# One third of a convolution moved to VectorE, seven taps instead of six on TensorE, and later copies of a projection in the prologue of a hybrid state-space block

## The reference

```python
xz = x @ in_proj_w.T                     # x group-normalised
xh, z = jnp.split(xz, 2, axis=-1)        # 192 channels each
xc = silu(conv3x3_depthwise(xh) + conv_b)
xs = [by rows, by columns, and both reversed]        # K = 4 directions
x_dbl = einsum('bkdl,kcd->bkcl', xs, x_proj_w)       # 24 + 16 + 16 rows
dts, Bs, Cs = split(x_dbl)
dts = softplus(einsum('bkrl,kdr->bkdl', dts, dt_projs_w) + dt_projs_b)
out_y = selective_scan(xs, dts, -exp(A_logs), Bs, Cs, Ds)
...
# then norm, gate by silu(z), projection, residual; linear attention; routed experts
```

## Time and profile before

| what | value |
|---|---|
| median of 3 runs | 2322.05 us (2319.41 to 2322.06) |
| the profiled execution | 2317.98 us, span 2316.2 us |
| busy over the span: PE, DVE, ACT, POOL | 87%, 68%, 50%, 56% |
| mean granted TensorE clock | 0.96 |
| the prologue | the first 283 us of the span |

### The profile page before, as it was taken

One profiled execution on the slowest core, in us unless ns is written; L12 is line 12 of the kernel. 1 busy time (PEld: TensorE's weight loads), 2 busy tenths in 40 slices (PEclk: granted clock), 3 DMA queues, 4 the chain that ended last, 5 costly groups with the idle time before them and its releaser, 6 DMA issues.

```text
span 2316.2 us, 20220 instructions
## 1 busy us (share of the span) xinstructions
PE 2019.9 (87%) x5878; PEld 934.3 (40%) x5878; DVE 1572.6 (68%) x1477; ACT 1153.9 (50%) x1251; POOL 1299.7 (56%) x467
## 2 busy tenths in 40 slices
PE   7997488888888888888888888779995999999997
PEld 3432133333333333333333333355662555555554
DVE  7697989999999999999999999453554000000000
ACT  4777766766667666676676766111111211111111
POOL 0100089999999999999999999301223111111110
PEclk9996589999999999999999999889997999999999
DMA  5545542222422224222232220510323433333300
GB/s 182 176 151 202 202 115 72 74 73 59 118 72 73 72 61 116 73 72 72 63 100 72 72 73 9 222 41 22 110 88 136 154 118 119 122 119 122 122 24 6
DMA packets 79203, 228.84 MB, mean 99 GB/s; under 512 B 10880, under 2 KB 37106, under 8 KB 77745
## 3 DMA queue, kind: packets, MB, share of 16 engines
q1 hardware_dynamic: 73008, 211.25, 28.4%
q0 software_dynamic: 6144, 16.98, 2.1%
HBM read 166.10 MB, written 64.03 MB: 99 GB/s over the span
## 4 chain that ended last, share of the span: by engine, by line
PE 47%; DVE 22%; issue 17%; POOL 8%; ACT 3%; DMA 1%; DVEq 0%; SPq 0%; ACTq 0%; POOLq 0%
DVE arena L1581 14%; PE ps L1375 11%; PE ps L1363 11%; PE ps L1116 6%; POOL arena L559 4%; POOL arena L542 4%; PE ps L1311 3%; PE ps L1100 2%; PE ps L1017 2%; PE ps L1045 2%; DVE ps L1564 1%; PE ps L1113 1%; PE ps L1262 1%; PE ps L1057 1%; PE ps L1300 1%
## 5 line engine op out<-in xcount | busy, mean ns | idle before, releaser
L559 POOL TENSOR_TENSOR arena<-arena 128x2048 f32<-128x2048 f32 x192 | 867.5, 4527 | 22.3 <-DVE arena L1581 18.4
L1116 PE MATMUL ps<-arena 128*128 128x512 f32 x1536 | 726.7, 595 | 29.0 <-POOL arena L559 28.9
L1581 DVE TENSOR_TENSOR_SCAN arena<-arena,ps 128x1024 f32<-128x1024 f32 x264 | 587.7, 2266 | 2.1 <-issue 2.1
L825 ACT ACTIVATE arena<-ps 128x1024 f32<-128x1024 f32 x384 | 390.7, 1018 | 255.9 <-PE ps L1100 248.1
L1100 PE MATMUL ps<-arena 96*128 (+1 forms) x1296 | 367.1, 385 | 133.9 <-DVE arena L1581 112.7
L1116 PEld LDWEIGHTS ps<-arena 128*128 128x128 f32 x1536 | 288.5, 190 | 288.4 <-issue 192.9
L542 POOL TENSOR_TENSOR arena<-arena 128x1024 f32<-128x1024 f32 x120 | 282.9, 2358 | 104.5 <-DMA arena<-b_rows 104.5
L1860 DVE TENSOR_TENSOR arena<-ps,arena 128x384 f32<-128x384 f32 x32 | 17.8, 557 | 449.1 <-PE ps L1375 449.1
L1564 DVE TENSOR_TENSOR ps<-ps,arena 128x1024 f32<-128x1024 f32 x264 | 309.1, 1216 | 16.0 <-PE ps L1100 15.9
L817 ACT ACTIVATE arena<-arena 128x1024 f32<-128x1024 f32 x264 | 300.8, 1139 | 8.9 <-DVE arena L1581 8.4
L1100 PEld LDWEIGHTS ps<-arena 96*128 96x128 bf16 x1296 | 112.9, 98 | 465.9 <-DVE arena L1581 215.7
(11 more groups left out here) (210 smaller groups left out, 1666.3 us busy)
## 6 DMA issues: line engine op xcount, KB each, us to landing
arena<-b_rows SPq DMA_DIRECT2D x240, 256.0 KB, 4.2
arena<-in_w SPq DMA_DIRECT2D x16, 2304.0 KB, 13.3
delta<-arena SPq DMA_DIRECT2D x24, 512.0 KB, 2.6
delta_x<-arena SPq DMA_DIRECT2D x24, 512.0 KB, 2.6
arena<-delta SPq DMA_DIRECT2D x24, 512.0 KB, 3.6
arena<-delta_x SPq DMA_DIRECT2D x24, 512.0 KB, 4.8
slot_in<-arena SPq DMA_DIRECT2D x8, 772.0 KB, 8.1
arena<-slot_in SPq DMA_DIRECT2D x8, 772.0 KB, 18.3
```

Of the source, the lines that this page charges most:

```text
L559: nc.gpsimd.tensor_tensor(hst[:, h:h + 2], hst[:, h:h + 2], c_sb[:, c:c + 2], ALU.mult).then_inc(p2_ok, 2)
L825: nc.scalar.activation(c_sb[:, u % RING], C_PS, ACT.Copy).then_inc(c_free, 1)
L1116: mm = pe.matmul(Y_PS[:, h * 512:(h + 1) * 512], ident, hst[:, u % HRING, h * 512:(h + 1) * 512], start=False, stop=(u == UN - 1))
L1581: nc.vector.tensor_tensor_scan(h, f, x, 0.0, ALU.mult, ALU.add).then_inc(sc_ok, 1)
```

## The change

It touches the prologue alone. Third 0 of pair 1 is convolved whole by VectorE (`first_third`), right behind pair 0's taps and around the first split, into the tile that `last_row` wrote before. TensorE's `conv` is left with thirds 1 and 2, of which it does seven taps, and VectorE's `last_taps` the remaining two. `x_proj(1, 0)` and its `split_hi` and `split_rest` stand ahead of the end of pair 0. `split_hi`, `split_rest`, `split_mid` and `split_lo` of the other projections stand one step later; TensorE's projections keep their steps. ScalarE does the three `conv_out` of pair 1 together, with one change of tables and one back instead of two and two. `FILL_ORDER` follows.

```diff
-TAPS, PE_TAPS = 9, 6
+TAPS, PE_TAPS = 9, 7
...
-for j in range(J):
-    FILL_ORDER += [("x", 0, j + 1), ("conv", 1, j)]
+FILL_ORDER += [("x", 0, 1), ("conv", 1, 1), ("x", 0, 2), ("x", 0, 3), ("conv", 1, 2)]
...
-CONV_AT = {1: (0, 0), 2: (0, 1), 4: (1, 0), 5: (1, 1), 7: (2, 0), 8: (2, 1)}
-LAST_ROW_AT = {2: 0, 5: 1, 8: 2}
-TWO_THIRDS_AT, LAST_THIRD_AT = 6, HALVES - 2
+CONV_AT = {1: (1, 0), 4: (1, 1), 7: (2, 0), 8: (2, 1)}
+LAST_TAPS_AT = {5: 1, 8: 2}
+SILU_AT, NEXT_PAIR_AT = HALVES - 3, HALVES - 2
+FAR_THIRD = place(3, 0) + 1
...
 # SP
-                    if i % J == 1 and i // J + 1 < K:
+                    if i % J == 2 and i // J + 1 < K:
                         store_parts(p, i // J + 1)
...
 # ScalarE
-                if p:
-                    split_hi(p, 0)
-                    split_mid(p, 0)
...
-                    if k < K and s % J == 0:
+                    if k < K and s % J == 1:
                         split_hi(p, k)
-                    if k < K and s % J == 1:
+                    if k < K and s % J == 2:
                         split_mid(p, k)
-                    if p == 0 and s == TWO_THIRDS_AT:
+                    if p == 0 and s == SILU_AT:
                         nc.scalar.preload_act_table_set("silu_and_others")
-                        conv_out(1, 0)
-                        conv_out(1, 1)
+                        for j in range(J):
+                            conv_out(1, j)
...
+                    if p == 0 and s == HALVES - 1:
+                        split_hi(1, 0)
+                    if p == 1 and s == 0:
+                        split_mid(1, 0)
...
 # TensorE
-                if p:
-                    x_proj(p, 0)
                 delta_product(p, 0)
...
+                    if p == 0 and s == NEXT_PAIR_AT:
+                        x_proj(1, 0)
...
 # VectorE
+            def first_third(first, last):
+
+                acc = xy[:, OJ, :].rearrange("p (h w) -> p h w", w=HW)
+                if first == 0:
+                    dve.wait_ge(xh_ok, FAR_THIRD)
+                    chain.link(nc.vector.tensor_scalar(acc, xpad[:, 0, 0:HW, 0:HW], conv_w[:, 0, 0:1], None, ALU.mult))
+                    first = 1
+                for tap in range(first, last):
+                    dy, dx = divmod(tap, 3)
+                    ins = nc.vector.scalar_tensor_tensor(out=acc, in0=xpad[:, 0, dy:dy + HW, dx:dx + HW], scalar=conv_w[:, 0, tap:tap + 1],
+                                                         in1=acc, op0=ALU.mult, op1=ALU.add)
...
-            for j in range(J):
+            for j in range(1, J):
                 for tap in range(PE_TAPS):
...
+            first_third(0, 7)
+            split_rest(0, 0)
+            first_third(7, 8)
+            split_lo(0, 0)
+            first_third(8, TAPS)
             for p in range(NP):
-                split_rest(p, 0)
-                split_lo(p, 0)
                 for s in range(HALVES + 1):
...
-                    if k < K and s % J == 0:
-                        split_rest(p, k)
                     if s >= 1:
                         finish(p, s - 1)
                     if k < K and s % J == 1:
+                        split_rest(p, k)
+                    if k < K and s % J == 2:
                         split_lo(p, k)
-                    if p == 0 and s in LAST_ROW_AT:
-                        last_row(LAST_ROW_AT[s])
+                    if p == 0 and s in LAST_TAPS_AT:
+                        last_taps(LAST_TAPS_AT[s])
+                    if p == 0 and s == HALVES - 1:
+                        split_rest(1, 0)
+                    if p == 1 and s == 0:
+                        split_lo(1, 0)
```

More of the change, by code:

```diff
@@ L200, in hybrid_block_kernel @@
         rw = Region(arena, PRO, COLS)
-        z_sb, xpad, conv_diag = rw.take(J, S), rw.take(J, PADW, PADW), rw.take(J, PE_TAPS, P)
+        z_sb, xpad, conv_diag = rw.take(J, S), rw.take(J, PADW, PADW), rw.take(J - 1, PE_TAPS, P)
         tap_sum = rw.take(2, S)
@@ L1029, in conv @@
                     mm = pe.matmul(slot[:, h * 512:(h + 1) * 512].rearrange("p (h w) -> p h w", w=HW),
-                                   conv_diag[:, j, tap], xpad[:, j, y0:y0 + HW // 2, dx:dx + HW],
+                                   conv_diag[:, j - 1, tap], xpad[:, j, y0:y0 + HW // 2, dx:dx + HW],
                                    start=(tap == 0), stop=(tap == PE_TAPS - 1))
@@ L1450, in taps, with last_taps @@
                         chain.link(ins)
-            def last_row(j):
+            def first_third(first, last):
[8 more added lines that the diff above has]
+                                                         in1=acc, op0=ALU.mult, op1=ALU.add)
+                    if tap == TAPS - 1:
+                        ins.then_inc(conv_ok, 1)
+                    else:
+                        chain.link(ins)
+            def last_taps(j):
                 slot = fill_slot("conv", 1, j).rearrange("p (h w) -> p h w", w=HW)
-                dve.wait_ge(cpe_ok, j + 1)
+                dve.wait_ge(cpe_ok, j)
                 for tap in range(PE_TAPS, TAPS):
@@ L1521, in _ @@
             nc.vector.tensor_scalar(a_neg, a_neg, A_LOG_MAX, None, ALU.min).then_inc(a_cut, 1)
-            for j in range(J):
+            for j in range(1, J):
                 for tap in range(PE_TAPS):
-                    nc.vector.tensor_scalar(conv_diag[:, j, tap], ident, conv_w[:, j, tap:tap + 1], None, ALU.mult)
+                    nc.vector.tensor_scalar(conv_diag[:, j - 1, tap], ident, conv_w[:, j, tap:tap + 1], None, ALU.mult)
             nc.vector.tensor_tensor(d_sum.rearrange("p q one -> p (q one)"), d_two[:, 0], d_two[:, 1], ALU.add).then_inc(setup, 1)
```

## The result

The changed kernel takes 2300.30 us (median, 2299.12 to 2300.90) against 2320.73 us for the kernel before in the same runs. The ratio is 0.9913, with a 95% interval of 0.9898 to 0.9927: 20.2 us faster by the ratio. The profiled execution took 2300.14 us with a span of 2298.3, 17.9 less than the profiled one of before, which was a quick one of its kind.

The account below looks back on a forecast made before the run. It took VectorE, ScalarE and TensorE as one loop locking each other, no engine at its limit; 187.6 to half 12 plus 73.6 for pair 1 put the scans at 261.2 instead of 282.90, 21.7 earlier: 2300.5 us, range 2294 to 2310.

Parts of the forecast that it names:

- The gap: VectorE's hole before half 0, 80.77 to 100.69: the eight taps fit with 4 us left and cost nothing.
- Stretch I: Pair 0, to the end of third 1's last taps: 146.18 less 8.01 of taps and waits, 138.2.
- Stretch II: Pair 0, on to third 2's last taps: they begin at 161.0 instead of 167.41, a gain of 6.4.
- the slot wait: In pair 0, x_proj(0, 3) waits for third 1's last tap to free its PSUM slot, at 138.2; VectorE waits 5.
- Stretch III: Pair 0, from third 2's last taps to half 12: 2.6+20.75+3.3 behind 161.0, so 187.6, between 184 and 190.
- The third hit: Before half 12, all three GpSimd copies would hold VectorE, not the two taken: the sum 1.6 us later.
- Stretch IV: Pair 1, half 12 to the scans: waits of 13.27 go, 1.25 and 2 come in, 83.59 becomes 73.6.
- The residue of 2: Pair 1, at half 14: VectorE's remaining wait for TensorE and ScalarE, 0 to 4 us, taken as 2.
- rival E: Half 12's or the copies' store lands behind four loads, or ScalarE waits 5 to 10 us: 2305 to 2310, chance 0.06.
- The tail: Behind VectorE's last halves: ten row loads and the last store, landing in 9.56, move with them.
- TensorE is loaded full: Pair 0: TensorE is busy 50.00 of 50 us from 100 to 150, at clock 1.00.
- Rival D: TensorE's clock stays low in pair 0's end and pair 1: 20.5 and 12 us lost, 2333, chance 0.05.

Follow-up runs that it names:

- the taps at step 4: Changed kernel with VectorE's last two taps of third 1 one step earlier (step 4 instead of 5): 0.9890 against the kernel before, 2293.28 us.
- Spreading the loads: Changed kernel with SP issuing the scans' loads singly behind the stores of pair 1's halves 1, 3, 5 and 7: 0.9908 against the kernel before, 2297.30 us.
- The copies alone: Kernel before with only the later split copies and the earlier x_proj(1, 0), convolution unchanged: 0.9915, 2298.62 us.
- the convolution alone: Kernel before with only the changed convolution and its three conv_out together, copies and x_proj(1, 0) unmoved: 0.9997, 2317.21 us.
- the combined version: Changed kernel with third 1's last taps at step 4 and the scans' loads spread over pair 1's stores: 0.9890 against the kernel before, 2293.14 us.

## Why the prediction was right, and where not

The forecast was 2300.5 and 2300.30 was measured. The total hides two steps that missed, and one credit that went to the wrong part.

- **The gap**: right. The eight taps end at 95.72, half 0 starts at 100.87 (100.69 before). The GpSimd copy stretched the first taps as allowed for: six of them take 9.50 and not 7.86, 1.6 us.
- **Stretch I**: forecast 138.2, measured 138.39. For TensorE the text names two projections and its sum has one, 5.35; the trace has one in that stretch too, at 112.87, so the sum is right.
- **Stretch II**: forecast 161.0, measured 163.00. The mechanism is as stated, the slot wait and a projection at the lower clock (8.19, I had averaged 5.35 and 7.94), but I took the middle of the term, and the measured value is 0.6 above even the upper end that I had worked out.
- **Stretch III**: 189.57-163.00 = 26.57, forecast 26.65. Two VectorE operations were held by GpSimd's three copies, 2.25 instead of 0.69 and 2.85 instead of 1.23, 3.2 us in all, as taken. The third hit, which I had drawn from the Trainium skill (SBUF — State Buffer, SBUF: two separate sides), did not come, and the rows say why. The page says this of VectorE operations with two SBUF inputs. During the first copy (163.32 to 165.30) VectorE did its two last taps, which read one of their inputs from PSUM, and these took 1.29 and 1.28 as without a copy. The page asks for no third hit there; I had counted the copies and not looked at which operations they meet. With the taps at step 4 three operations were held.
- **Stretch IV**: forecast 73.6, measured 265.25-189.57 = 75.68. The residue of 2 was 3.71, and not for what I named: it was rival E's mechanism, the store of half 12, smaller than the 5 to 10 us given there. I had put half 16 some 20 us behind it and called that enough; half 12's store was issued 1.6 us after its `finish` ended (196.45+1.23) and took 10.89 to land. Spreading the loads removed it, which shows the cause.
- **The tail** moved with the end of the halves within a microsecond, as said. That it was no fixed length but the landing of one store was in the earlier trace rows for me to see.

Together the steps missed by 4.1 us; the measured difference of medians, 20.4, is larger than the 17.65 of the two profiled executions, so that the forecast looks better than its sum was. From profile to profile the prediction has 2296.3, and 2300.14 was measured. That the total came out within 0.2 us is luck.

The step of the argument that failed is the credit. I counted five taps, 6.4 us, as a gain of stretches I and II beside the waits of the copies. I did set 5 us of waiting at the slot against them, so the sum held, but I did not see that this left the convolution's part with nothing. The copies alone gave as much as both, the convolution alone nothing: its taps are paid back in the waits of 3.02 and 3.74, and only with the slot wait shortened do they give their 5 to 6 us. And "TensorE is loaded full" in pair 0 was true and no argument: it stayed full in the version with the copies alone, and VectorE still did not wait. What bound the loop was that ScalarE came to a copy whose projection was not ready, with the next half's operations queued behind it, and VectorE likewise to `split_rest`. The runs moved both together, so which of the two counts for more is not shown. Rival D did not come: the clock's mean was 0.86 and 0.85 in the two windows and 0.67 from 200 to 250 (0.70 before), and every projection of the changed kernel took 5.4 to 8.2 us. In pair 1 a projection took 6.67 to 6.99 from start to end, less than twice 5.35, so the clock rose while it ran. The Trainium skill's statement (TensorE: Matmul & The Clock Gate, Part 1) that activity releases the throttle agrees with this; a fall of the clock that it does not explain stands in the last section.

What stays open: why the projection behind 1.51 us of idle time still ran at the lower clock. It cost nothing, which the combined version shows: there TensorE came to `x_proj(0, 3)` without a pause and did it in 5.42 us (133.62), and half 12 started 83.01 us behind half 0, against 83.05 with step 4 alone and the pause. Whether six or seven taps are better is below what was measured. The medians of the kernel before lay between 2317.5 and 2320.7 in the four sets of runs.

## What to carry to other kernels

An in-order engine should not stand at an operation whose input is still being made while it has others ready. Here it was worth 19.7 us to move such operations one step later and to start one projection sooner, and nothing to remove five operations from the engine that ends last. In the version with the copies alone TensorE was busy for all 50 us from 100 to 150, and VectorE, which ends last, did not wait; look for the rows in which others wait before you call a full engine the bound. And where a stage ends in stores that the next one waits for, look at what was put in the same queue ahead of the last of them.

## What the runs showed of the hardware that was not expected

- A pause of 1.51 us of TensorE in front of a projection was followed by 8.39 us for its 12 records, nearly the same as behind a pause of 8.50 (8.19); at full clock they take 5.42. That the pause did it is not shown, for the clock also fell without one. In the combined version TensorE is busy without a break from 86 to 100 us, and the granted clock is 0.99 until 98 and 0.50 (the 1.2 GHz level) from 98 to 100, behind two delta products, which use 48 rows:

```profile
94.13 3.70 PE L1056 MATMUL ps<-arena 48*128 48x512 f32 x8
97.76 7.10 PE L1044 MATMUL ps<-arena 128*128 128x512 f32 x12
```

- A VectorE TENSOR_SCALAR with one SBUF input was stretched from 0.69 to 2.25 us while GpSimd copied, like the operations with two SBUF inputs. Taps with one input in SBUF and one in PSUM were not (1.29 and 1.28).
- A store of 512 KB behind the loads of the scans landed after 10.89 us instead of the 2.7 that is the median of all stores of this kind, and with six loads of 256 KB taken from in front of the last store it landed 7.1 us after its issue instead of 11.0.
